# Narrow matmuls of two inner products alternated with the wide ones of an outer product, in a 31x31 depthwise convolution on one Trainium2 core

## What is computed

```python
def _gn(v, G=32, eps=1e-05):
    g = v.reshape(B_, G, C_ // G, H_, W_)
    m = jnp.mean(g, axis=(2, 3, 4), keepdims=True)
    s = jnp.var(g, axis=(2, 3, 4), keepdims=True)
    return ((g - m) / jnp.sqrt(s + eps)).reshape(v.shape)
...
x = x + _L0_conv_ref(_gn(x), L0_conv_weight, L0_conv_bias_term)          # 31x31, depthwise
x = x + _L1_conv_ref(_gn(x), L1_conv_weight_coord, L1_conv_radius, L1_conv_weights)   # 11x11, depthwise
```

## Time and profile before

| | us |
|---|---|
| median of 3 runs | 3515.29 (3515.28 to 3515.53) |
| the profiled execution | 3515.18 |
| its span in the trace | 3513.4 |
| PE busy | 3427.3 (98%) |
| PEld busy | 3265.2 (93%) |
| DVE busy | 3146.1 (90%) |
| ACT, POOL busy | 1299.3 (37%), 1202.2 (34%) |
| DMA queue 1, share of 16 engines | 86.3% |

### The profile page before, as it was taken

How to read it: one execution, slowest core, us unless ns; L and a number is a source line. 1 busy time by engine, 2 the same in 40 slices (tenths; PEclk the granted TensorE clock), 3 DMA queues, 4 the chain that set the end, 5 groups by cost and what they waited for, 6 DMA issues and landing times.

```text
span 3513.4 us, 66359 instructions
## 1 busy us (share of the span) xinstructions
PE 3427.3 (98%) x21312; PEld 3265.2 (93%) x21312; DVE 3146.1 (90%) x4671; ACT 1299.3 (37%) x1637; POOL 1202.2 (34%) x840
## 2 busy tenths in 40 slices
PE   5899999999999999999999999999999999999997
PEld 4789999999999999999999999999999999999996
DVE  7899998899988999988999988999989999889988
ACT  3333333333333333333333333333333333333333
POOL 6213333333333333333333333333333333333332
PEclk9999999999999999999999999999999999999999
DMA  8998888898888898888898898988888988889774
GB/s 181 187 200 160 172 161 166 175 181 166 163 169 168 165 177 171 160 165 173 172 173 169 161 166 173 184 165 163 169 168 163 182 168 160 165 170 186 136 147 89
DMA packets 896128, 587.51 MB, mean 167 GB/s; under 512 B 501656, under 2 KB 858136, under 8 KB 895576
## 3 DMA queue, kind: packets, MB, share of 16 engines
q1 hardware_dynamic: 895416, 585.62, 86.3%
q10 hardware_dynamic: 544, 0.38, 0.1%
HBM read 499.20 MB, written 86.61 MB: 167 GB/s over the span
## 4 chain that ended last, share of the span: by engine, by line
PE 92%; issue 3%; SPq 2%; DVE 2%; DMA 1%; POOL 0%; ACT 0%; DVEq 0%; POOLq 0%; ACTq 0%
PE acc L1302 92%; SPq L554 2%; DMA toep<-padded 1%; DVE yt L1088 0%; DVE acc L1079 0%; DVE raw L1097 0%; DMA padded<-raw 0%; DVE x_lo L1062 0%; ACT toep L953 0%; DVE x_lo L1056 0%; SPq L568 0%; SPq L594 0%; DVE raw L1134 0%; SPq L578 0%; DVE acc L1119 0%
## 5 line engine op out<-in xcount | busy, mean ns | idle before, releaser
L1302 PE MATMUL acc<-x_hi,toep 128*112 128x224 f32 (+5 forms) x14208 | 3303.6, 323 | 79.1 <-DMA toep<-padded 70.4
L1302 PEld LDWEIGHTS acc<-x_hi,toep 128*112 128x112 f32 x14208 | 2381.1, 182 | 188.6 <-issue 79.9
L1302 PE MATMUL acc<-x_lo,toep 128*112 128x224 f32 (+5 forms) x7104 | 2299.4, 324 | 0.0
L1302 PEld LDWEIGHTS acc<-x_lo,toep 128*112 128x112 f32 x7104 | 1289.7, 182 | 52.2
L793 POOL TENSOR_TENSOR xt<-xt 128x960 f32<-128x960 f32 x188 | 425.7, 2264 | 1118.9 <-DVE xt L1037 1118.9
L830 ACT ACTIVATE x_hi<-xt 128x768 fp32r<-128x768 f32 (+1 forms) x384 | 279.2, 727 | 1092.4 <-POOL xt L789 578.7
L1079 DVE TENSOR_TENSOR acc<-acc,yt 128x896 f32<-128x896 f32 x384 | 418.9, 1091 | 220.6 <-PE acc L1302 219.5
L788 POOL TENSOR_TENSOR xt<-xt 128x512 f32<-128x512 f32 x180 | 233.1, 1295 | 1094.5 <-DVE xt L1037 1094.5
L833 ACT ACTIVATE x_hi<-xt 128x960 fp32r<-128x960 f32 x384 | 386.9, 1007 | 572.3 <-POOL xt L793 323.1
L1037 DVE STREAM_TRANSPOSE xt<-images 128x960 f32<-128x960 f32 x384 | 452.5, 1178 | 34.8 <-ACT images L817 6.6
L817 ACT ACTIVATE images<-raw,norm 128x896 f32 (+1 forms) x384 | 439.8, 1145 | 88.1 <-DVE norm L1017 88.1
(11 more groups left out here) (59 smaller groups left out, 412.7 us busy)
## 6 DMA issues: line engine op xcount, KB each, us to landing
toep<-padded SPq DMA_DIRECT2D x384, 322.0 KB
toep<-padded SPq DMA_DIRECT2D x384, 273.0 KB
toep<-padded SPq DMA_DIRECT2D x384, 217.0 KB
out_dram<-raw SPq DMA_DIRECT2D x189, 336.0 KB, 5.6
raw<-in_x_dram SPq DMA_DIRECT2D x93, 672.0 KB, 11.7
toep<-padded SPq DMA_DIRECT2D x768, 58.5 KB
toep<-padded SPq DMA_DIRECT2D x384, 80.5 KB
toep<-padded SPq DMA_DIRECT2D x384, 47.2 KB
```

The costliest lines, as they stand in the source:

```text
L1302: last = nc.tensor.matmul(dst, stationary, src[:, cols], start=(m == matrices[0][0] and part == 0 and src is x_hi), stop=(m == matrices[-1 ...
```

## The change

Only the PE program of `convolve` changes, and in effect only for FIRST jobs (for a SECOND job the list `beside` is empty and the order is as before). The matmuls, their operands, banks and count are the same. Of a FIRST job's three inner products the first is run alone; then come the two waits; then each of the 24 matmuls of the second and third inner product (bank 3) is followed by one of the 24 matmuls of the first outer product (bank 1); the second outer product (bank 2) follows alone. `u_done` is signalled by the last matmul of bank 3, wherever it now stands.

```diff
                 before_outer = 3 if f.halved else 1
-                for k, (bank, column, start, shift, held, count, matrices) in enumerate(f.products()):
-                    if k == before_outer:
-                        pe.wait_ge(lo_ready, n + 1)
-                        if positive(n + 1 - P_RING):
-                            pe.wait_ge(image_ready, n + 1 - P_RING)
...
+                products = [list(steps(k, *product)) for k, product in enumerate(f.products())]
+                outer_steps = [x for product in products[before_outer:] for x in product]
+                alone = 1 if f.halved else len(products[:before_outer])
+                beside = [x for product in products[alone:before_outer] for x in product]
+                for product in products[:alone]:
+                    for x in product:
+                        multiply(*x)
+                pe.wait_ge(lo_ready, n + 1)
+                if positive(n + 1 - P_RING):
+                    pe.wait_ge(image_ready, n + 1 - P_RING)
+                for k, x in enumerate(outer_steps):
+                    if k < len(beside):
+                        multiply(*beside[k])
+                    multiply(*x)
```

More of the change, by code:

```diff
@@ L1283, in convolve, with steps @@
                 before_outer = 3 if f.halved else 1
-                for k, (bank, column, start, shift, held, count, matrices) in enumerate(f.products()):
-                    if k == before_outer:
-                        pe.wait_ge(lo_ready, n + 1)
-                        if positive(n + 1 - P_RING):
-                            pe.wait_ge(image_ready, n + 1 - P_RING)
+                def steps(k, bank, column, start, shift, held, count, matrices):
                     def outputs(m):
@@ L1298, in convolve, with multiply @@
                         for part, src in ((0, x_hi), (0, x_lo), (1, x_hi)):
[L1299 to L1306, removed]
+                            yield (dst, w, part, src[:, cols], m == matrices[0][0] and part == 0 and src is x_hi,
+                                   m == matrices[-1][0] and part == 1, done[k])
+                def multiply(dst, w, part, moving, first, last, signal):
+                    block = last_place(i, s)
+                    stationary = (toeplitz(toep, f, place_of_toep, part, w) if block is None
+                                  else last_toeplitz(block, part, w))
+                    ins = nc.tensor.matmul(dst, stationary, moving, start=first, stop=last, skip_group_check=True)
+                    if last and signal is not None:
+                        ins.then_inc(signal, 1)
+                products = [list(steps(k, *product)) for k, product in enumerate(f.products())]
[12 more added lines that the diff above has]
+                    multiply(*x)
             def iteration(i):
```

## The result

| | before | changed |
|---|---|---|
| median, us | 3515.41 | 3571.11 |
| runs, us | 3515.28 to 3516.7 (4) | 3570.04 to 3572.14 (4) |
| span of the profiled execution, us | 3513.4 | 3569.2 |

The changed kernel is slower by 55.7 us: a ratio of 1.0157, 95% interval 1.0145 to 1.017. Forecast were 3567 us, in a range of 3536 to 3600. The profiled execution took 3570.98 us.

A forecast was written before the change was run, and what follows sets the result against it. PE's own pace was taken to bound the kernel in 91% of the span. Alternation counted 0 and the stalls from the moved waits +52 us: 3515.18 + 52 = 3567 us, range 3536 to 3600.

The forecast's parts named there:

- The bound: In the steady stretch, 91% of the span, only PE's own pace counts; DVE's busy time is 10% short of it.
- Step 1: Narrow matmuls take 0.105 us each; a 192 is held by something other than its columns, 12 ns perhaps recoverable.
- Step 2: In alternating pairs, loads go one ahead only, so a wide neighbour hides nothing: 0.105 + 0.20 us a pair, gain 0.
- Loads hidden: Rival: in alternating pairs narrow matmuls find their loads done, 192s take 92 ns; -27.6 us, 3539 us; chance 0.17.
- Fixed part goes: Rival: alternated narrow matmuls lose the fixed 13 ns or so above their columns; -81 us, 3486; chance 0.07.
- Banks cost: Rival: changing bank with each matmul costs 5 to 10 ns a pair; 23 to 46 us, 3590 to 3613; chance 0.10.
- Step 3: Waits moved from 37th to 13th matmul make PE wait for L1062 at slots 4 and 10: 60 x 0.865 = +52 us.
- Step 4: Moved signals do no harm: `u_done` goes from 3.8 to 8.0 us into the job, L1069 doesn't wait, slot 6's 0.64 us shrinks.

The follow-up runs named there:

- the residual last: Changed kernel with DVE doing the normalisation's last steps and L1062 first at slots 2 and 8, the residual sum behind them; 3518.81 us.
- 96 columns: Kernel before with 96 instead of 112 columns in each stationary operand, output rows 48 to 55 not computed; 3458.23 us.
- The waits alone: Kernel before, its order of matmuls kept, only the two waits moved from the 37th matmul of a FIRST job to the 13th; 3567.6 us.
- The kernel with waits at the head: Kernel before, its order of matmuls kept, with the two waits moved to the head of each FIRST job; 3772.43 us.
- the kernel with L1062 early: Kernel before with both waits at the head of each FIRST job and L1062 ahead of the normalisation's end at slots 2 and 8; 3621.84 us.

## Why the prediction was right

- **The bound** (PE alone): held. In the steady stretch PE waits for nothing but DVE's x_lo in any alternated version, and for nothing at all in the kernel before; the 3518.8 us with the residual last show that DVE's 90% are no bound.
- **Step 1**, narrow matmuls cost 0.105 us whatever their width, 192s held by something: right to 3 ns (0.103 and 0.106), and that it goes with the load's columns is now shown. Its 12 ns to be had per 192 came out with 96 columns.
- **Step 2**, a wide neighbour hides nothing: right in the sum of a pair, not in its parts. It said that the wide matmul comes 0.105 us behind a narrow one, and named 0.105 us for each alternated narrow one as a sign of being right; a 192 took 0.088, and its wide neighbour the 0.018 us more. Taken was 0; 20 ns a job was measured, 4 us. "Loads hidden" would have been -27.6 and is refuted twice, by the kernel without stalls (3518.8, not 3488) and by the loads, which still start 102 ns apart. "Fixed part goes" (3486) falls with it. "Banks cost" had set 23 to 46 us; a loss of 4 us is there, a twelfth to a sixth of it, but that it is the banks' isn't shown.
- **Step 3**, 60 stalls of 0.86 and 0.88 us at slots 4 and 10: 59 of 0.85 and 0.88 us are in the trace, and the one at the start, of about 0.7. The waits alone gave 3567.6 against 3567. The chain on DVE was as rigid as taken: it started with PE's end of slot 2, and what PE lost in one stall it never got back in the next.
- **Step 4**, slot 6 gets no worse, `u_done` harmless: right; slot 6 took 12.480 us and L1069 has no wait for PE.
- **What was missed**: the 4 us of alternation itself, all of the 4 us between 3567 and 3571. The term was put at 0 from a single seam read to 0.01 us, which can't show 1 ns a pair; that it came out so small was not known beforehand.

The Trainium skill's page "TensorE: Matmul & The Clock Gate" ("HAM oscillation — how this bites in real kernels") warns that idle gaps between bursts of matmuls put the clock back to half; its example has waits of 3 to 5 us. The kernel with waits at the head agrees in kind, but there 1.9 to 2.1 us idle were enough in 53 of 59 cases, with 0.187 us a matmul behind them instead of 0.105. In the changed kernel itself the granted clock stayed at 1.00 behind the pauses of 0.6 us, so the rule adds nothing to its 56 us.

## What to carry to other kernels

A wait that costs nothing in the trace still has a cover, and an edit to the order of matmuls that moves the wait spends it: take the end of the awaited instruction less the start of the job, from the trace, for every slot, not on the mean, since here two slots of six made all but one of the stalls. In this kernel a load was covered only by the one matmul ahead of it (loads 102 ns apart over a narrow matmul, whatever stood next to it), so mixing narrow and wide ones didn't average load time over both; what helped a narrow matmul was a shorter load. And a repair on a loaded helper engine (L1062 ahead of the normalisation) can hand the lateness on to the next slot: look for the new wait before calling it free.

## What was not expected of the hardware

- A pause of PE of 1.9 to 2.1 us, in a stream that is otherwise dense, was followed by the half clock in 53 of 59 cases (0.52 granted in the window shown, 224-column matmuls 0.187 us apart instead of 0.105) and then cost 1.5 us more, three quarters of the pause again; pauses of 1.5 us in the kernel with L1062 early and 0.6 us in the changed kernel left the clock at 1.00.
- At the half clock the 192s are 0.187 us apart too, as the 224s: what holds a 192 takes longer at the lower clock too.
- Alternating the two outer products matmul by matmul, each with its own bank and operands, costs about half a nanosecond a matmul (23 to 26 ns on 48), unevenly over the widths.
- The record of a matmul can start before its weights are there, as far as the starts tell: behind a 192 the wide one is on record after 88 ns, where loads start 102 ns apart.
